# A four-phase float32 kernel: the first transform step of its front phase, as three float32r passes instead of one float32 pass

## What is computed

```
u = x @ W_in + b_in                       # 8192 x 512 by 512 x 1536
uc = short_conv(u, short_w, short_b)      # three taps along the sequence
x0, x1, v = split(uc, 3);  v = v * x1
k = gen_filter(...)                       # sine network, 64 hidden features, then W3
v = irfft(rfft(pad(v)) * conj(rfft(k)))[:8192] + bias
y = (v * x0) @ W_out + b_out
```

## Time and profile before

| | |
|---|---|
| time, 3 runs | 2384.0 us median (2382.87 to 2387.05) |
| profiled execution | time 2374.5 us, span 2372.7 us |
| PE busy over the span | 1991.1 us (84%) |
| DVE busy | 1494.4 us (63%) |
| ACT busy | 971.9 us (41%) |
| POOL busy | 279.8 us (12%) |
| granted TensorE clock, mean | 0.908 (1.00 in the chunks of the front phase) |

### The profile page before, as it was taken

One profiled execution on the slowest core, in us unless ns is written; L12 is line 12 of the kernel. 1 busy time (PEld: TensorE's weight loads), 2 busy tenths in 40 slices (PEclk: granted clock), 3 DMA queues, 4 the chain that ended last, 5 costly groups with the idle time before them and its releaser, 6 DMA issues. The chain is left out here.

```text
span 2372.7 us, 34849 instructions
## 1 busy us (share of the span) xinstructions
PE 1991.1 (84%) x12336; PEld 1401.1 (59%) x12336; DVE 1494.4 (63%) x2800; ACT 971.9 (41%) x1756; POOL 279.8 (12%) x151
## 2 busy tenths in 40 slices
PE   6999999999999799999959999997566666676444
PEld 5777777777776355555528998896545353252100
DVE  3878778778776466666647888886234335354343
ACT  3444444444443344444435555554323223232222
POOL 1100100100010000000005555451000000000000
PEclk9999999999999899999989999998789878687555
DMA  4133334233332899999977777774889899999999
GB/s 145 60 112 132 111 107 138 103 111 130 106 111 108 240 256 258 259 258 260 260 207 242 244 242 238 229 243 164 313 309 340 342 378 365 409 333 405 380 392 342
DMA packets 309644, 556.45 MB, mean 235 GB/s; under 512 B 27775, under 2 KB 120159, under 8 KB 301154
## 3 DMA queue, kind: packets, MB, share of 16 engines
q1 hardware_dynamic: 300258, 537.45, 67.9%
q10 hardware_dynamic: 9216, 16.78, 1.9%
HBM read 314.67 MB, written 205.91 MB: 219 GB/s over the span
## 5 line engine op out<-in xcount | busy, mean ns | idle before, releaser
L89 PE MATMUL p_pu<-p_xT_high,p_win_high 128*128 128x512 f32 (+1 forms) x816 | 334.6, 410 | 23.5 <-POOL p_xT_low L84 23.2
L91 PE MATMUL p_pu<-p_xT_low,p_win_high 128*128 128x512 f32 (+1 forms) x816 | 318.1, 390 | 0.0
L90 PE MATMUL p_pu<-p_xT_high,p_win_low 128*128 128x512 f32 (+1 forms) x816 | 318.1, 390 | 0.0
L369 ACT ACTIVATE p_t<-p_pu,p_tbias,p_taps 128x512 f32<-128x512 f32 x192 | 149.4, 778 | 385.0 <-PE p_pu L91 384.0
L473 DVE SCALAR_TENSOR_TENSOR p_t<-p_halo,p_taps,p_t 128x128 f32<-128x128 f32 (+1 forms) x384 | 197.2, 518 | 136.3 <-ACT p_t L369 135.2
L473 DVE SCALAR_TENSOR_TENSOR p_t<-p_pu,p_taps,p_t 128x384 f32<-128x384 f32 (+1 forms) x384 | 210.3, 548 | 6.8
L89 PEld LDWEIGHTS p_pu<-p_xT_high,p_win_high 128*128 128x128 f32 x816 | 154.9, 190 | 56.4 <-issue 29.2
L91 PEld LDWEIGHTS p_pu<-p_xT_low,p_win_high 128*128 128x128 f32 x816 | 154.3, 189 | 34.4
L1410 DVE COPY e_taken<-e_pd 128x1024 f32<-128x1024 f32 x64 | 78.4, 1225 | 151.8 <-PE e_pd L1343 151.5
L90 PEld LDWEIGHTS p_pu<-p_xT_high,p_win_low 128*128 128x128 f32 x816 | 155.0, 190 | 27.4
L1355 PE MATMUL e_pd<-e_taken,e_ff 128*32 128x128 f32 x2048 | 86.4, 323 | 94.7 <-DMA e_ff<-in_L_ffn_f 91.0
(11 more groups left out here) (119 smaller groups left out, 3822.7 us busy)
## 6 DMA issues: line engine op xcount, KB each, us to landing
s_I<-e_out SPq DMA_DIRECT2D x64, 1024.0 KB, 8.1
s_SV<-p_sout SPq DMA_DIRECT2D x128, 256.0 KB, 2.0
q_av<-s_SV SPq DMA_DIRECT2D x64, 512.0 KB, 4.3
q_v_x<-q_v SPq DMA_DIRECT2D x128, 256.0 KB, 4.2
s_Z<-q_z SPq DMA_DIRECT2D x128, 256.0 KB, 3.4
o_zin<-s_Z SPq DMA_DIRECT2D x64, 512.0 KB, 3.6
e_ff<-in_L_ffn_f SPq DMA_DIRECT2D x64, 512.0 KB, 8.5
e_inter<-s_I SPq DMA_DIRECT2D x32, 1024.0 KB, 12.4
```

The costliest lines, as they stand in the source:

```text
L89: pe.matmul(out, a[0], b[0], start=start, stop=False)
L90: pe.matmul(out, a[1], b[0], start=False, stop=False)
L91: return pe.matmul(out, a[0], b[1], start=False, stop=stop)
L369: nc.scalar.activation(t[r][m % 2][:], pu[(W + n) % 3][:], ACT.Identity, bias=tbias[:, w:w + 1], scale=taps[:, w, 2:3]).then_inc(t_ok, 1)
```

## The change

`v`, the features and the table are now each kept as two float32r tiles, high and low (a rounded value, and what the rounding left), and a stage is six float32r products, three of 128x512 and three of 128x64. For this, ACT's copy of `pv` writes the high part, and a new DVE operation `low_vt` writes the low part; `keep_ht` gets a second DVE operation for the low part. The table comes in already split and so twice as large: it is copied from the input to a scratch tensor in DRAM and from there loaded. `keep_hs` writes its result once rather than twice side by side, and `store_h` then writes it to the two places with four transfers instead of two. The raw `W_in` is loaded into the space of the two halo buffers instead of a tile of its own.

```diff
-        win = sb("win", [P, DT, 3 * D])
+        halos = sb("halo", [P, 2, W, HC])
+        halo = [halos[:, s] for s in range(2)]
+        win = halos[:].rearrange("p s w c -> p (s w c)").rearrange("p (k w) -> p k w", k=DT)
-        vt = [sb(f"vt{s}", [P, J, D]) for s in range(2)]
-        dft = [sb(f"dft{s}", [P, J, 2, P]) for s in range(2)]
+        vt = [[sb(f"vt_{n}{s}", [P, J, D], F32R)[:] for n in ("high", "low")] for s in range(2)]
+        dft = [sb(f"dft{s}", [P, J, 2, 2, P], F32R)[:] for s in range(2)]
...
+            def copy_dft(i):
+                c = slice(i * J, (i + 1) * J)
+                sp.dma_start(S["DFT"][:, c], A["dft1s"][:, c]).then_inc(dft_st[i % 2], 16)
...
-                pe.matmul(pz[n % 2][:], dft[i % 2][:, j, r, :], vt[i % 2][:, j, :], start=True, stop=True
-                          ).then_inc(s_ps, 1)
-                o = pe.matmul(p_h[:, r * J + j, :], dft[i % 2][:, j, r, :], ht[i % 2][:, j % 2, j // 2, :],
-                              start=True, stop=True)
+                table = [dft[i % 2][:, j, h, r, :] for h in range(2)]
+                product(pe, pz[n % 2][:], table, [h[:, j, :] for h in vt[i % 2]], start=True, stop=True
+                        ).then_inc(s_ps, 1)
+                o = product(pe, p_h[:, r * J + j, :], table, [h[:, j % 2, j // 2, :] for h in ht[i % 2]],
+                            start=True, stop=True)
...
-                nc.scalar.copy(vt[i % 2][:, :, k * P:(k + 1) * P], pv[:]).then_inc(vt_ok, 1)
+                split_high(nc.scalar.copy, vt[i % 2][0][:, :, k * P:(k + 1) * P], pv[:]).then_inc(vt_high, 1)
...
+            def low_vt(m):
+                i, c = m // DT, slice(m % DT * P, (m % DT + 1) * P)
+                dve.wait_ge(vt_high, ONE + m + 1)
+                if i >= 2:
+                    dve.wait_ge(s_ps, ONE + (i - 1) * STAGES)
+                split_low(dve, vt[i % 2][1][:, :, c], pv[:], vt[i % 2][0][:, :, c]).then_inc(vt_ok, 1)
...
-                dve.tensor_copy(hs[i % 2][:], p_h[:].rearrange("p (j a) h -> p j a h", a=1).to_broadcast(
-                    [P, 2 * J, 2, HID])).then_inc(hs_ok, 1)
+                dve.tensor_copy(hs[i % 2][:], p_h[:]).then_inc(hs_ok, 1)
...
                 if i == NCH:
+                    for m in range(NCH * DT - 2, NCH * DT):
+                        low_vt(m)
                     break
                 for x in range(W):
                     taps_add(i, x)
+                    if x % 3 == 0 and i * DT + x // 3 >= 2:
+                        low_vt(i * DT + x // 3 - 2)
```

More of the change, by code:

```diff
@@ L142, in front_phase @@
         h1, h2 = sb("h1", [P, HC]), sb("h2", [P, HC])
-        ht = [sb(f"ht{s}", [P, 2, 2, HID]) for s in range(2)]
-        hs = [sb(f"hs{s}", [P, 2 * J, 2, HID]) for s in range(2)]
+        ht = [[sb(f"ht_{n}{s}", [P, 2, 2, HID], F32R) for n in ("high", "low")] for s in range(2)]
+        hs = [sb(f"hs{s}", [P, 2 * J, HID]) for s in range(2)]
         pu = [ps(f"pu{s}", [P, CH]) for s in range(3)]
@@ L158, in front_phase @@
                                     "ht_ok", "h_ps", "hs_ok"))
-        pos_in, dft_in, x0_st, hs_st = ([sem(f"p_{n}{s}") for s in range(2)] for n in
-                                        ("pos_in", "dft_in", "x0_st", "hs_st"))
+        pos_in, dft_in, x0_st, hs_st, dft_st = ([sem(f"p_{n}{s}") for s in range(2)] for n in
+                                                ("pos_in", "dft_in", "x0_st", "hs_st", "dft_st"))
+        vt_high, ht_high = sem("p_vt_high"), sem("p_ht_high")
         s_st = [sem(f"p_s_st{s}") for s in range(NS)]
@@ L190, in load_dft @@
                     sp.wait_ge(h_ps, ONE + i - 1)
-                sp.dma_start(dft[i % 2][:], A["dft1"][:, i * J:(i + 1) * J]).then_inc(dft_in[i % 2], 16)
-            sp.dma_start(win[:], A["W_in"].rearrange("(k p) w -> p k w", p=P)).then_inc(w_in, 16)
+                sp.wait_ge(dft_st[i % 2], ONE + (i // 2 + 1) * 16)
+                sp.dma_start(dft[i % 2].bitcast(F32), S["DFT"][:, i * J:(i + 1) * J]).then_inc(dft_in[i % 2], 16)
+            sp.dma_start(win, A["W_in"].rearrange("(k p) w -> p k w", p=P)).then_inc(w_in, 16)
             load_x(0)
@@ L209, in _ @@
                 load_pos(i)
+            load_x(1)
+            for i in range(2):
+                copy_dft(i)
+            for i in range(2):
                 load_dft(i)
-            load_x(1)
             def store_x0(m):
@@ L225, in store_h @@
                 for r in range(2):
-                    sp.dma_start(S["SH"][:, r * N2 + i * J:r * N2 + (i + 1) * J, :].rearrange("p j (a h) -> p j a h", a=2),
-                                 hs[i % 2][:, r * J:(r + 1) * J]).then_inc(hs_st[i % 2], 16)
+                    at = S["SH"][:, r * N2 + i * J:r * N2 + (i + 1) * J, :]
+                    for a in range(2):
+                        sp.dma_start(at[:, :, a * HID:(a + 1) * HID], hs[i % 2][:, r * J:(r + 1) * J]
+                                     ).then_inc(hs_st[i % 2], 16)
             for i in range(NCH + 1):
@@ L242, in _ @@
                         load_dft(i)
+                    if x == 6 and i + 2 < NCH:
+                        copy_dft(i + 2)
             store_h(NCH - 1)
@@ L437, in _ @@
             dve.wait_ge(halo_ok, ONE + W)
-            dve.tensor_copy(halo[0][:].rearrange("p w (a n) -> p w a n", a=2)[:, :, :, 0],
+            dve.tensor_copy(halo[0].rearrange("p w (a n) -> p w a n", a=2)[:, :, :, 0],
                             nbin[:].rearrange("p (w a) -> p w a", a=1).to_broadcast([P, W, 2])).then_inc(ready, 1)
@@ L495, in keep_ht @@
                     dve.wait_ge(h_ps, ONE + i - 1)
-                dve.tensor_copy(ht[i % 2][:].rearrange("p b h j -> p (b h j)"), pf[:, 1, :]).then_inc(ht_ok, 1)
+                high, low = (h[:].rearrange("p b h j -> p (b h j)") for h in ht[i % 2])
+                split_high(dve.tensor_copy, high, pf[:, 1, :]).then_inc(ht_high, 1)
+                dve.wait_ge(ht_high, ONE + i + 1)
+                split_low(dve, low, pf[:, 1, :], high).then_inc(ht_ok, 1)
+            def low_vt(m):
[4 more added lines that the diff above has]
+                split_low(dve, vt[i % 2][1][:, :, c], pv[:], vt[i % 2][0][:, :, c]).then_inc(vt_ok, 1)
             def keep_hs(i):
@@ L1544, in constants, with rounded @@
     c["dft1"] = np.stack([re, im], axis=2)
+    def rounded(v):
+        bits = v.astype(f).view(np.uint32)
+        return ((bits + 0x7FF + (bits >> 12 & 1)) & np.uint32(0xFFFFF000)).view(f)
+    high = rounded(c["dft1"])
+    c["dft1s"] = np.stack([high, rounded(c["dft1"].astype(f) - high)], axis=2)
     back = np.stack([2 * np.cos(th), -2 * np.sin(th)], axis=0) / 256
```

8 lines of the change are left out of this document (4 added, 4 removed).

## The result

The changed kernel takes 2400.18 us (median of 10 runs, 2390.3 to 2402.94). The kernel before, run beside it, takes 2383.66 (10 runs, 2380.58 to 2389.5). The ratio is 1.0061, 95% interval 1.0047 to 1.0075: about 14.5 us slower. The forecast had the sign and, for the full chunks, the mechanism; the sum said 7.7, about half. The profiled execution took 2400.94 us, span 2399.1. That is 26.4 more than the profiled execution before, but 8.5 us of the difference lie outside the front phase, in lines that the diff does not touch (the experts' phase alone differs by 4.5). So the phase's own rows come first, and the ratio is kept apart from them.

What follows compares the result with a forecast made beforehand. PE was taken to bound the front phase; stages -6.5, stall +11.5, last pass +1.9 and phase's end +0.8 gave +7.7 us, 2391.7 on the median, given as 2391.5. Own range 2388 to 2397; 8 in 10, 2380 to 2400.

Steps and rivals of the forecast that it cites:

- PE sets the pace: Front phase, 15 full chunks of 45.53 us: PE is busy throughout at full clock and bounds them.
- The stage: PE's stage of six products: 1.03 us instead of 1.09, narrow passes 0.11 apart; -6.5 us over 128 stages.
- Rival 2: Stages: narrow passes cost more than a weight load, at 0.22 each 2434 us, at 0.15 each 2407; chance 0.08.
- rival 3: Stages: fast weight loads make a narrow pass some 0.03 us and a stage 0.79; 2361 us; chance 0.03.
- The stall at x = 4: Passes 1 to 15: stage 0, behind unit x = 4, waits 0.77 us for DVE's low part; +11.5 us.
- rival 4: Stage 0's stall is half as large, 0.4 us, 6 us in all; 2386 us; chance 0.20.
- Rival 1: Stage 0: DVE's low part is not late, so there is no stall; 2378 us; chance 0.10.
- End of the phase: From the last `keep_hs` to the next phase: shorter copy -0.6, four issues +0.8, small packets +0.6; together +0.8 us.
- the 0.6 for small pieces: Phase's end: storing the features in 256-byte packets adds 0.6 us, from nothing below to 5 above.
- Edits at nothing: Table copy and doubled load, added issues in each chunk, raw `W_in` in the halo buffers: no cost.
- This lag is gone by x = 10, and no stage waits for these two blocks: Low parts at x = 6 and 9 fall in DVE's idle time, despite POOL blocking additions; no cost.
- The last pass. +1.9 us: Last pass: the last turn and stage 0 wait for `low_vt`, so stage 0 runs at 768.2 instead of 766.35.

Runs made afterwards that it cites:

- e1: The changed kernel with the low part of the chunk's last block made ahead of the additions of x = 3, not behind them: 2385.57 us, ratio 1.0006.
- e8: The kernel before with only the narrow `keep_hs` copy and four stores of 256-byte pieces: 2385.59 us, ratio 1.0005.
- e4: The changed kernel without `low_vt`, the third wide product reading v's high part again: 2385.34 us, ratio 0.9998.
- e3: The changed kernel with unread products filling PE's idle time in the last pass: 2394.62 us, ratio 1.0035.
- e6: The changed kernel with e1, e2, unread products in the last pass and its second last `low_vt` ahead of `keep_hs`: 2379.33 us, ratio 0.9977.
- e10: e6 without the unread products in the last pass: 2383.57 us, ratio 1.0002 to the kernel before.
- e9: e6 with `low_vt` ahead of the additions at x = 9 as well: 2381.37 us, ratio 0.9992 to the kernel before.
- e2: The changed kernel with the low part at x = 6 made between the third and fourth addition: 2396.9 us, ratio 1.0044.
- e7: The kernel before with unread products in PE's idle time of the last pass: 2382.24 us, ratio 0.9991.
- e5: The kernel before with one unread DVE operation added ahead of the last gate, to lengthen PE's idle time: 2385.6 us, ratio 1.0004.

## Why the prediction was right in kind and short in size

**The size, and where luck helped.** On the median that the forecast used (2384.0) the ratio of 1.0061 makes 2398.5. That is above the forecast's own range, 2388 to 2397, and inside the wide one, to 2400. The wide range's upper part was put there for dear small transfers and dearer narrow passes, and neither came. What filled it, the first chunk and the clock, stands in no rival, so that the wide range held is luck.

**PE sets the pace: right.** After, in the stretch of the earlier trace rows:

```profile
394.00:438.00 44.00, 43.54 (x205) 34.91 (x204) 36.40 (x73) 19.34 (x37) 4.60 (x1) 1.00 0.45 141
```

PE is busy for 43.54 of 44 us at full clock.

**The stage: right.** 1.02 to 1.03 as priced, narrow passes 0.11 apart. Rival 2, 0.22 a pass, and rival 3, a stage of 0.79, are both ruled out by 767.32, 767.43, 767.54 and by the stage's 1.02. The faster load that the Trainium skill ("TensorE: Matmul & The Clock Gate", "Weight-path perf modes") gives to weights that are not float32 does not show for the float32r weights of this trace. The kernels without a stall show the saving alone: 45.53 - 45.10 = 0.43 a chunk, for 8 x 0.05 = 0.40.

**The stall at x = 4: right.** 0.77 forecast, 0.76 measured, at the product named and for DVE's L84; rival 4, half of it, fell. Rival 1's "a low part made there at once, not behind the additions, would be in time" is e1 word for word, but the kernel as changed doesn't do it.

**End of the phase: right as a sum, by two errors that cancel**: +0.83 for +0.8 (alone +0.95, e8). Four issues cost 1.39 us more, not 0.8, and the 0.6 for small pieces is a term that came out as nothing: 3.79 and 3.82 us from the last issue to `q_ones`, for 3.82. **Edits at nothing: right.** In the waits of after PE has none for `dft` or for a store.

**"This lag is gone by x = 10, and no stage waits for these two blocks": the step that failed first.** It holds in the 13 full chunks between. It was read from a chunk in the middle and never from the first, and it asked only who waits at a stage. What waits is the turn of the next block. The interval's +4.5 is 2.4 of idle time (e1 against e4), 0.76 of the stall of i = 1, less 0.1 for the stages, and 1.5 that are left for the clock. The low part itself isn't blocked by POOL: in a middle chunk, with POOL busy from 432.81 to 437.41, DVE shows

```profile
433.25 0.69 DVE L84 TENSOR_TENSOR p_vt_low<-p_pv,p_vt_high 128x512 fp32r<-128x512 f32 x1 [0.77 <-ACT p_vt_high L79]
434.50 3.06 DVE L488 SCALAR_TENSOR_TENSOR p_t<-p_halo,p_taps,p_t 128x128 f32<-128x128 f32 x1 [0.56 <-ACT p_t L384]
```

the one with an operand in PSUM runs in its usual time, the one with both operands in SBUF takes 3.06 for 0.35. The Trainium skill ("GPSIMD Engine Reference", "Specifications") names this kind, a DVE instruction with two SBUF inputs, as one that contends with GpSimd; the trace agrees (3.06 us for 0.35). It is the order alone that puts `low_vt` behind such an addition.

**"The last pass. +1.9 us": the term that was mis-sized.** The delays were right: the idle times grew by 1.37 and 0.72, 2.1 together, for the 1.9. But the term held the stages at the earlier trace rows's distance, that is at full clock. In after they stood 1.92 apart, and the phase's last piece grew by 7.2. With the clock held it grew by 1.6 (e3: 78.62 for 77.05), where 1.8 was forecast; the other 5.6 are the clock. That this was the clock's fall and no other cost is shown by e3 (the same idle time filled, -6.2 us in the time) and by e6 against e10 (6.3 us in the profiles). The profile of before had PE idle for 2.75 us with the clock held, and this was taken as how the place behaves; e4 and e8 show that it may as well fall.

No step of the prediction spoke of the clock in this pass.

**The sum on the median.** The phase's rows give 16.7 us more, the ratio 14.5. The profiled execution of before kept its clock in the last pass and lies 9.5 us under its median. If some of its timed runs lost it, as e8's profile did, they paid up to 3 us of the last pass already. This is argued, not shown: no timed run has a trace.

**What stays open:** how often the kernel before loses its clock there; why the fall lasted longer under split stages (last section); whether the clock made the 1.5 us that are left in the first interval; and how much of e6's gain is above e9's 0.1%.

## What to carry to other kernels

When an edit adds work to a queue, check each of its places in the first and the last round as well as in a full one: the slack that was read in the middle (2.08 us before x = 7) is not there where PE has fewer products between two units. A result that another engine needs soon goes to the place in the order where its input is ready, not behind the work that happens to stand there: moving one instruction gave back 13 us, 11.4 of them by the stall. And where the tensor engine stands idle for a few us ahead of a serial tail, price the tail at half clock as well as at full, and try a few unread products in the gap.

## What the hardware showed that was not expected

The same idle time of PE ended in both ways. PE's longest waits in i = 0 and in the last pass, with the granted clock behind them, one profiled execution of each kernel:

| idle us | clock stayed at 1.00 | clock fell to half |
|---|---|---|
| 0.2 to 0.9 | e2, e6, e10 (i = 0); e3, e6, e7, e9 (last pass) | none |
| 2.75 to 2.83 | e1 (i = 0); before (last pass) | after, e3 (i = 0); e4, e8 (last pass) |
| 3.52 to 4.28 | none | e10, after, e1, e2, e5 (last pass) |

And a fall did not cost the same. From the turn of the last block to the last `keep_hs`, with the clock held, 10.2 us (before, e7) and 10.5 (e3, e6, e9); with a fall, 12.8 and 13.2 in front of float32 stages (e5, e8), and 15.3 to 17.3 in front of the split ones (after, e1, e2, e4, e10). At half clock a float32 stage takes 2.13 to 2.19 us from start to start (e5, e8) and a split one 1.92, so the price of a stage is not what differs. It is the length of the fall: in stretches of 0.5 us, the clock is at half for about 7 us in e5 and e8, about 14 in after, e1, e2 and e10, and 17 in e4. In e4 and e10 PE was busy for the whole of 765 to 775 and the clock was 0.50 throughout. Split products alone are not the reason: the units of i = 0 are split products as well, and there the fall (after, e3) lasted 3.4 us. What the stages of the last pass have beside them, narrow passes and no other work, was not varied. Why, no run here tells. The Trainium skill ("TensorE: Matmul & The Clock Gate", "Part 1: The HAM clock gate") says, of the rise to full clock when products begin, that its point varies from run to run with the same kernel. No kernel was traced twice here, so no run shows it; the table's middle row, where six idle times of the same length ended in both ways, does not speak against it. Unread products in an idle stretch of 3 to 4 us were worth about 6 us in a tail of 10 (after against e3, e10 against e6). That is nearly as much as the change's cheaper stages save in the whole phase (0.43 us in each of 16 chunks).
